# Zeroed dummy matmuls at the start, bf16 rounding sums and merged rotary products in a two-layer Perceiver block

## What is computed

```
x = x + L0_xattn(layernorm(x), ctx)    # 16 heads of 128, inputs rounded to fp8, 512 context keys per batch
x = x + L0_attn(layernorm(x))          # causal convolution, state-space scan
x = x + L0_ffn(layernorm(x))           # 8 experts, top 2
x = x + L1_xattn(layernorm(x), ctx)    # plain attention over the context with a mask
x = x + L1_attn(layernorm(x))          # 16 small heads with rotary positions
x = x + L1_ffn(layernorm(x))           # weights looked up in a 16-entry table
```

```python
def _div_clamp_fp8(x, scale):
    y = jnp.clip(x.astype(jnp.float32) / scale, -FP8_MAX, FP8_MAX)
    y = y.astype(jnp.bfloat16).astype(jnp.float32)
    return y.astype(jnp.float8_e4m3fn).astype(jnp.float32)
```

## Time and profile before

| | us |
|---|---|
| three runs | 454.0, 456.86, 457.67 |
| median | 456.86 |
| the profiled execution | 454.53 |
| its span, first to last instruction | 453.0 |

### The profile page before, as it was taken

How to read it: one execution, slowest core, us unless ns; L and a number is a source line. 1 busy time by engine, 2 the same in 40 slices (tenths; PEclk the granted TensorE clock), 3 DMA queues, 4 the chain that set the end, 5 groups by cost and what they waited for, 6 DMA issues and landing times.

```text
span 453.0 us, 6836 instructions
## 1 busy us (share of the span) xinstructions
PE 422.0 (93%) x2399; PEld 295.6 (65%) x2401; DVE 364.0 (80%) x764; ACT 254.6 (56%) x794; POOL 26.4 (6%) x34
## 2 busy tenths in 40 slices
PE   4999999999999999999999999998987899878587
PEld 1453445777885766767676775876574799836386
DVE  5789999858898879699899988976888799567731
ACT  2468888676545886758987486593113372231150
POOL 0000000000300000101001010100100021000000
PEclk9999999999999999999999999999999899999899
DMA  8268110424001114893446643893558879230000
GB/s 303 116 228 330 35 59 1 187 89 169 1 0 51 43 46 117 172 310 75 116 116 130 171 88 60 199 295 156 113 103 271 322 257 239 55 117 1 2 1 23
DMA packets 14047, 58.57 MB, mean 129 GB/s; under 512 B 1792, under 2 KB 2496, under 8 KB 12480
## 3 DMA queue, kind: packets, MB, share of 16 engines
q1 hardware_dynamic: 10992, 41.66, 25.1%
q0 software_dynamic: 3024, 16.52, 18.5%
HBM read 41.40 MB, written 0.26 MB: 92 GB/s over the span
## 4 chain that ended last, share of the span: by engine, by line
PE 74%; DVE 17%; ACT 4%; issue 2%; DMA 1%; SPq 0%; DVEq 0%; ACTq 0%
PE PS L458 12%; PE PS L431 10%; PE PS L433 9%; PE PS L432 9%; PE PS L1760 4%; PE PS L478 3%; PE PS L1097 3%; DVE small_dt.float L2059 2%; PE PS L1224 2%; PE PS L505 2%; PE PS L1079 2%; PE PS L467 2%; PE PS L1833 1%; PE PS L1082 1%; DMA raw_dt.float<-in_wk_nat 1%
## 5 line engine op out<-in xcount | busy, mean ns | idle before, releaser
L579 ACT ACTIVATE sq_dt.float<-PS 128x128 bf16<-128x128 f32 x256 | 67.1, 278 | 33.5 <-PE PS L433 27.0
L458 PE MATMUL PS<-s_dt.float,ctx_ring_dt.float 128*128 128x512 f32 x128 | 57.7, 593 | 1.3 <-DVE px_dt.float L813 1.3
L431 PE MATMUL PS<-wkc_dt.float32r,ctx_hi_dt.float32r 128*128 128x512 f32 x128 | 53.6, 419 | 0.4
L579 ACT ACTIVATION_READ_ACCUMULATOR sq_dt.float<-PS 128x1 f32 x256 | 53.4, 209 | 0.0
L433 PE MATMUL PS<-wkc_dt.float32r,ctxT_ring_dt.float32r 128*128 128x512 f32 x128 | 50.3, 393 | 0.0
L432 PE MATMUL PS<-wkT_dt.float32r,ctx_hi_dt.float32r 128*128 128x512 f32 x128 | 50.2, 392 | 0.0
L1760 PE MATMUL PS<-wch_dt.float,xs_dt.float 128*128 128x512 f32 x96 | 42.0, 592 | 0.0
L458 PEld LDWEIGHTS PS<-s_dt.float,ctx_ring_dt.float 128*128 128x128 f32 x128 | 23.6, 190 | 25.0 <-issue 23.0
L656 ACT ACTIVATE luttmp_dt.float<-low_bit_dt.float,vec_dt.float,small_dt.float 128x1536 f32<-128x1536 uint8 x24 | 38.5, 1654 | 2.0 <-DMA lutw_dt.float<-luttmp_dt.float 2.0
L663 DVE SCALAR_TENSOR_TENSOR luttmp_dt.float<-idx_dt.float,luttmp_dt.float 128x1536 f32<-128x1536 uint8 x21 | 36.4, 1749 | 0.0
L431 PEld LDWEIGHTS PS<-wkc_dt.float32r,ctx_hi_dt.float32r 128*128 128x128 f32 x128 | 24.0, 188 | 12.2 <-ACT sq_dt.float L579 7.7
(11 more groups left out here) (307 smaller groups left out, 866.2 us busy)
## 6 DMA issues: line engine op xcount, KB each, us to landing
lutw_dt.float<-luttmp_dt.float POOLq DMA_DIRECT2D x21, 768.0 KB, 6.2
wch_dt.float<-in_chunks SPq DMA_DIRECT2D x6, 1024.0 KB, 6.2
ctxT_ring_dt.float<-in_ctxT SPq DMA_DIRECT2D x8, 512.0 KB, 3.4
ctx_ring_dt.float<-in_ctx SPq DMA_DIRECT2D x8, 512.0 KB, 4.0
keysT_dt.float<-in_ctxT SPq DMA_DIRECT2D x8, 512.0 KB, 7.5
keys_dt.float<-in_ctx SPq DMA_DIRECT2D x8, 512.0 KB, 7.6
luttmp_dt.float<-in_idx SPq DMA_DIRECT2D x3, 768.0 KB, 6.0
zu_dt.float<-in_wproj SPq DMA_DIRECT2D x1, 2048.0 KB, 7.3
```

What stands on the lines that cost most here:

```text
L431: nc.tensor.matmul(o, x_hi, hi[:, c, :], start=c == 0, stop=False)
L458: last = nc.tensor.matmul(bank(5 + c), keysr[k][:, t, c * 128:c * 128 + 128], sS[k][:, t, :], start=t == 0, stop=t == KT - 1)
L579: last = nc.scalar.activation(sq[:, (4 * hf + g) * D:(4 * hf + g + 1) * D], bank(hf)[:, g * D:(g + 1) * D], ACT.Square, accum_out=ssq[:, k ...
```

## The change

Four edits, none of which changes what the kernel returns beyond rounding:

1. GpSimd first zeroes 256 fp32 words of the scratch `sq`. TensorE waits for that and not for the constants, runs 14 dummy matmuls of 512 bf16 columns on the zeros, then waits for the constants, transposes x, and runs three dummies of the old kind on the constants.
2. The constant `ROUND` goes from 1.5·2^20 to 1.5·2^4, so that the sum fits bf16, and the sum is written in place over the bf16 value in `round_fp8`, `quantize_values` and `quantize_heads`. In `scaled_input` the difference stays bf16 too, and the multiplication by the input scale reads it and writes fp32. The fp32 scratch `t_q` is gone.
3. As the sum now overwrites a buffer that an earlier difference still reads, VectorE gets waits on its own `catx_ready` and `catc_ready` in `read_values`, `quantize_heads` and `quantize_core`.
4. `pad_half` becomes one copy instead of two, `rotate_keys` one product instead of two, `rotate_queries` one instead of four.

```diff
-ROUND = 1.5 * 2.0 ** 20
+ROUND = 1.5 * 2.0 ** 4
...
         def round_fp8(step, n, dst):
...
             step(nc.vector.tensor_scalar(m_bf[:, 0:n], m_bf[:, 0:n], FP8_MIN_NORMAL, ROUND, ALU.max, ALU.mult))
-            step(nc.vector.tensor_tensor(dst, y_bf[:, 0:n], m_bf[:, 0:n], ALU.add))
-            return nc.vector.tensor_tensor(dst, dst, m_bf[:, 0:n], ALU.subtract)
+            step(nc.vector.tensor_tensor(y_bf[:, 0:n], y_bf[:, 0:n], m_bf[:, 0:n], ALU.add))
+            return nc.vector.tensor_tensor(dst, y_bf[:, 0:n], m_bf[:, 0:n], ALU.subtract)
...
             def read_values(p, hf):
                 dve.wait_ge(v_full, 2 * p + hf + 1)
+                if p or hf:
+                    dve.wait_ge(catx_ready, 2 * p + hf)
...
-                self_step(nc.vector.tensor_tensor(t_q, y_q, m_q, ALU.add))
-                nc.vector.tensor_tensor(dst, t_q.rearrange("p (a q) -> p a q", a=8),
+                self_step(nc.vector.tensor_tensor(y_q, y_q, m_q, ALU.add))
+                nc.vector.tensor_tensor(dst, y_q.rearrange("p (a q) -> p a q", a=8),
...
             def quantize_heads(b, nb, heads):
+                dve.wait_ge(catx_ready, 6 if b == 6 else 7 + heads.start // 8)
...
-                self_step(nc.vector.tensor_tensor(t, y, m, ALU.add))
-                nc.vector.tensor_tensor(catx[:, heads, b * S:(b + 1) * S], t.rearrange("p (a q) -> p a q", a=n),
+                self_step(nc.vector.tensor_tensor(y, y, m, ALU.add))
+                nc.vector.tensor_tensor(catx[:, heads, b * S:(b + 1) * S], y.rearrange("p (a q) -> p a q", a=n),
...
             def pad_half(j):
                 dve.wait_ge(turned, j + 1)
-                o = bank(TURNED[1, j], CT, 128)
-                for c in range(CT):
-                    last = nc.vector.tensor_copy(hpad[:, c, 4 * j:4 * j + 4, 3:S + 3],
-                                                 o[:, c, :].rearrange("p (b s) -> p b s", b=4))
-                return last
+                return nc.vector.tensor_copy(hpad[:, :, 4 * j:4 * j + 4, 3:S + 3], bank(TURNED[1, j], CT, 4, S))
...
             def rotate_keys(j):
...
-                nc.vector.tensor_tensor(k1, o1, cos, ALU.mult)
-                step(nc.vector.tensor_tensor(k2, o2, sin, ALU.mult))
+                both = kr_kt2[:, :, t].rearrange("p a (b s) -> p a b s", b=4)
+                turns = consts[:, CONST["cos"].start:CONST["sin"].stop].rearrange("p (a s) -> p a s", a=2)
+                step(nc.vector.tensor_tensor(both, bank(KEYED[j], 4, 4, S)[:, 0:2],
+                                             turns.unsqueeze(2).broadcast_to([128, 2, 4, S]), ALU.mult))
                 nc.vector.tensor_tensor(kr[:, t], kr[:, t], kt2[:, t], ALU.add)
             def rotate_queries(j):
...
-                for a in range(4):
-                    last = nc.vector.tensor_tensor(qr[:, a, t].rearrange("p (b s) -> p b s", b=4),
-                                                   bank(ASKED[j], 4, 4, S)[:, a], mixed, ALU.mult)
-                last.then_inc(rot_ready, 1)
+                nc.vector.tensor_tensor(qr[:, :, t].rearrange("p a (b s) -> p a b s", b=4), bank(ASKED[j], 4, 4, S),
+                                        mixed, ALU.mult).then_inc(rot_ready, 1)
...
+            pe.wait_ge(warm_ready, 1)
+            for _ in range(14):
+                nc.tensor.matmul(bank(0), sq[:, 0:128], sq[:, 0:512], start=True, stop=True)
             pe.wait_ge(ld_const, 16)
-            keep_clock(2, 0)
             pe.wait_ge(ln_done, 1)
...                                             # four transposes of x
             last.then_inc(x_turned, 1)
+            keep_clock(3, 0)
...
         def _(pool):
             step = Steps(pool, pool_step)
+            nc.gpsimd.memset(buf("sq", 256), 0.0).then_inc(warm_ready, 1)
...
             def scaled_input(n, turned):
...
-                step(round_fp8(step, CT * T, xs[:, n].rearrange("p c t -> p (c t)")))
+                step(round_fp8(step, CT * T, y_bf[:, 0:CT * T]))
                 for c in range(CT):
-                    last = nc.vector.tensor_scalar(xs[:, n, c, :], xs[:, n, c, :], col("in_scale", n * CT + c), None,
+                    last = nc.vector.tensor_scalar(xs[:, n, c, :], yv[:, c, :], col("in_scale", n * CT + c), None,
                                                    ALU.mult)
...
             def quantize_core(n):
                 dve.wait_ge(y_core, n + 1)
+                if n:
+                    dve.wait_ge(catc_ready, n)
```

More of the change, by code:

```diff
@@ L218, in build @@
         low_full, low_read = sem("low_full"), sem("low_read")
+        warm_ready = sem("warm_ready")
         ld_vec, x_turned, x_read, lnT_kept, chunk_read = (sem(n) for n in ("ld_vec", "x_turned", "x_read", "lnT_kept",
@@ L298, in build @@
         y_q, e_q, m_q = (buf("qtmp", 512, skip=256 * i, dtype=bf16) for i in range(3))
-        t_q = buf("qtmp", 512, skip=768)
         def round_fp8(step, n, dst):
@@ L856, in quantize_heads @@
             def quantize_heads(b, nb, heads):
+                dve.wait_ge(catx_ready, 6 if b == 6 else 7 + heads.start // 8)
                 n = heads.stop - heads.start
-                y, e, m, t = (v[:, 0:n * S] for v in (y_q, e_q, m_q, t_q))
+                y, e, m = (v[:, 0:n * S] for v in (y_q, e_q, m_q))
                 self_step(nc.vector.tensor_tensor(y.rearrange("p (a q) -> p a q", a=n), bank(nb, NH, S)[:, heads, :],
@@ L940, in build @@
         kr, kt2 = buf("rotact", T, skip=2048), buf("rotact", T, skip=2304)
+        kr_kt2 = buf("rotact", 2, T, skip=2048)
         vr = buf("rotact", TT, 256, skip=2560)
@@ L1602, in rotate_keys @@
                 dve.wait_ge(qkv_full, 3 * j + 1)
-                k1, k2 = (v[:, t].rearrange("p (b s) -> p b s", b=4) for v in (kr, kt2))
-                o1, o2 = (bank(KEYED[j], 4, 4, S)[:, a] for a in range(2))
-                cos, sin = (const(name).unsqueeze(1).broadcast_to([128, 4, S]) for name in ("cos", "sin"))
-                nc.vector.tensor_tensor(k1, o1, cos, ALU.mult)
-                step(nc.vector.tensor_tensor(k2, o2, sin, ALU.mult))
+                both = kr_kt2[:, :, t].rearrange("p a (b s) -> p a b s", b=4)
+                turns = consts[:, CONST["cos"].start:CONST["sin"].stop].rearrange("p (a s) -> p a s", a=2)
+                step(nc.vector.tensor_tensor(both, bank(KEYED[j], 4, 4, S)[:, 0:2],
+                                             turns.unsqueeze(2).broadcast_to([128, 2, 4, S]), ALU.mult))
                 nc.vector.tensor_tensor(kr[:, t], kr[:, t], kt2[:, t], ALU.add)
@@ L1611, in rotate_queries @@
                 t = slice(128 * j, 128 * j + 128)
-                mixed = const("mixed").unsqueeze(1).broadcast_to([128, 4, S])
+                mixed = const("mixed").unsqueeze(1).unsqueeze(1).broadcast_to([128, 4, 4, S])
                 dve.wait_ge(qkv_full, 3 * j + 2)
-                for a in range(4):
-                    last = nc.vector.tensor_tensor(qr[:, a, t].rearrange("p (b s) -> p b s", b=4),
-                                                   bank(ASKED[j], 4, 4, S)[:, a], mixed, ALU.mult)
-                last.then_inc(rot_ready, 1)
+                nc.vector.tensor_tensor(qr[:, :, t].rearrange("p a (b s) -> p a b s", b=4), bank(ASKED[j], 4, 4, S),
+                                        mixed, ALU.mult).then_inc(rot_ready, 1)
             def rotary_shift(j):
```

## The result

The changed kernel takes **452.62 us** (median of 20 executions, 450.07 to 456.89) against 457.02 us for the kernel before beside it (20 executions, 454.0 to 459.78): ratio **0.993, 95% interval 0.991 to 0.995**. The ratio leaves out one disturbed execution of the changed kernel (456.89 us). It lies near the quotient of the means (452.95 and 456.39 us, 0.992) and not near that of the medians (0.990): by the ratio the gain is 3.3 us, by the medians 4.4. The forecast was 451.8 us with a range of 449.6 to 455.0. The 0.7% of the ratio lies within 1%, to which the prediction gave 0.46, and not above, to which it gave 0.50; by the medians it is 1.0%. The profiled execution took 451.98 us, its span 450.5 us. That is 2.55 us less than the profiled execution before. Where the rest of the gain went is the subject of half the experiments.

What follows compares the result with a forecast made beforehand. It took TensorE as the main bound (74% of the span), with VectorE on the chain mostly from 19 to 63 us. Terms of -3.0, -0.6, -0.2 and -0.5 summed to -4.3 us; forecast 451.8 us, range 449.6 to 455.0.

Steps and rivals of the forecast that it cites:

- The dummies: At the start, early dummies raise TensorE's clock by 8.5 us, so the centring ends at 11.96 instead of 14.95: -3.0 us.
- the bound that the prediction used: At the start, the fourteen dummies end at 7.2 us if TensorE's clock stays low, sooner if it rises under them.
- The rival of the late rise: TensorE's clock rises only in the middle of the centring: half the gain, -1.5 us, giving 453.3 us; chance 12%.
- that of the useless zeros: Zeros do nothing for the clock and the dummies delay the centring 1.1 us: 454.8 us profiled, 457 against the median; 6%.
- going below the median: Forecast set at 451.8 us, between 450.2 from the profiled execution and 452.6 from the median of the runs.
- The bf16 sums: VectorE's sums of 512 columns take 0.43 instead of 0.69 us; `scaled_input` on the chain gives -0.6 us, ends 0 and -0.7.
- capped `scaled_input(2)`: In the front, this call ends in a TensorE wait of only 0.19 us, so no more of its saving passes.
- `quantize_core`, `quantize_values`: In the loop, VectorE saves 2.1 and 1.6 us, but TensorE is busy 99.8% there: 0 on the total.
- `quantize_heads`, the waits and `pad_half`: Shorter 256-column sums with the added waits counted: -0.2 us; one copy instead of two in `pad_half`: -0.08 us twice.
- `rotate_queries`: Behind the loop, one product of 0.69 us replaces four taking 0.87: -0.18 us twice, both on the chain.
- all starts move 4 us, and drops may fall in heavier or lighter stretches: Rival that TensorE's clock drops at another place, near 354 to 358 or 425 us: ±1.5 us on every case; no chance given.
- the forecast sum: All parts together: -3.0 - 0.6 - 0.2 - 0.5 = -4.3 us, 0.9% of the profiled time.

Runs made afterwards that it cites:

- the repeat: The changed kernel, unedited, run once more beside the kernel before: median 452.2 us over six executions, ratio 0.990; its profiled execution took 450.93 us.
- the kernel with the old start: The changed kernel with two dummies on the constants in place of the fourteen on zeros, and without the three before the centring: 454.01 us, ratio 0.996.
- the 52 and 26 above: Executions with a recorded mean granted clock, 52 of the kernel before and 26 of the changed one: at high clock 454.5 and 452.1 us, at low 457.6 and 454.6.
- the version with all of them filled: The changed kernel with the GpSimd mask conversion later and dummies in TensorE's idle gaps behind the loop: median 450.25 us over six executions, ratio 0.985.

## Why the prediction was nearly right

**The dummies: right, size -2.7 for -3.0.** In the profiled execution the rise came earlier than I had to assume, at about 4.1 us, so the dummies ended at 5.82 us and not at 7.2; in the repeat they did end at 7.24 us, the bound that the prediction used, and the centring took the same 3.70 us. The centring went from 6.43 to 3.70 us. I had counted eight intervals of 0.43 us; the step also holds the end of the last product. `scaled_input(0)` was ready at 10.97 us, 0.85 us ahead of need, and VectorE's idle at 16 us was still 0.92 us. The rival of the late rise and that of the useless zeros fell with the weight loads. The rise at 7.05 us in the repeat, 1.3 us ahead of the centring, and the kernel with seven dummies show that the first was not far off. Another 0.40 us of the 3.13 is luck: `wkn` landed that much sooner, and I had said that no edit moves it. For going below the median I had argued that the slow start can be worse in one run than in another; the three traces with a slow centring don't bear that out (6.43, 6.33 and 6.43 us).

**The bf16 sums: mechanism right, front under-sized, -1.0 for -0.6.** The estimate for 512 columns, 0.43 us, was measured as 0.42. The column part halved, 0.53 to 0.27 us for 512 columns, which is the rate that the prediction cited. Wrong were two parts of the step. The multiplications that read bf16 and write fp32 cost nothing extra (350 ns in both kernels, I had put +0.12 on two). And I capped `scaled_input(2)` at the 0.19 us of idle that the trace printed; breaking the transposes there had cost 0.46 us from start to start. The idle printed before a group understated the wait here (0.50 for 0.55 and 0.19 for 0.46 us): the ends of matmuls are modelled and can cover part of it. The starts of the next group tell it.

**`quantize_core`, `quantize_values`: 0, right.** 7.77 us in both, 0.53 us less work a call notwithstanding.

**`quantize_heads`, the waits and `pad_half`: -0.38 for -0.36.** The 256-column sums took 0.29 us for 0.43 (0.30 forecast); with them in fp32 the stretch was 0.21 us longer, which leaves 0.17 for `pad_half` (0.16 forecast). From the first difference to the next read it is 0.74 us before and after, so the added waits cost nothing.

**`rotate_queries`: 0.87 to 0.68 us, as forecast.** The stretch around it is 0.39 us shorter, but the clock moved within it too (0.86 and 0.80 at 420 to 430 us before, 0.56 and 0.75 after), so its share is not shown.

**What failed: "all starts move 4 us, and drops may fall in heavier or lighter stretches", at ±1.5.** The size was fair (+1.64 in the profiled pair), the treatment as luck alone was not enough. I had not asked what the drop at 354 to 358 us held up and what it held back. Reading who released GpSimd's mask conversion (TensorE's third gate and up product) beside VectorE's routing would have shown that full pace in these products brings two engines into one lock, +0.76 us. It is not the moved start that does this: the kernel with the old start did it too. Against the profiled execution the parts give 454.53 - 3.1 - 1.0 - 0.4 - 0.4 = 449.6; with 0.76 and 1.64 given back, 452.0, which is what it took (451.98). Over many executions the change is worth 3.3 us by the ratio and 4.4 by the medians; the forecast sum was 4.3. The sums in the front gave 0.4 us more than that sum has and the centring 0.3 less, and if those executions are like the 52 and 26 above, the 4.4 holds a difference in mean clock which no term of the sum has, so part of the agreement is chance. How often each course occurs in either kernel is open: a course can be told only in a profiled execution, and of the kernel before there is one, of the changed kernel two.

## What to carry to other kernels

Dummy matmuls on a scratch that needs no load are worth their place where the first real products run at half pace; give them enough to come close to the first real work (here fourteen, with gaps of about 1 us behind them; seven, with 2.56 us, were too few), and check the pace at the start by the distance of the weight loads, not by the printed clock. Look at more than one execution: the clock rose at 4.1 us in one and at 7 us in another of the same program. Before you fill TensorE's idle to hold its clock, find every gap of the tail: in two profiles with gaps left the drop only moved on, and the version with all of them filled is the one that came out below the changed kernel on the same chip; and where a drop comes ahead of the filling, the dummies stand in the queue. Compare a single profiled pair only stretch by stretch, since one program can take two courses that differ by 2.4 us in 18.

## What the runs showed of the hardware

- TensorE's clock rose on products of zeros, 14 bf16 products of 512 columns in a row: at about 4.1 us in the changed kernel and at about 7 us in its repeat; in all ten traces that had the fourteen it was up before the centring. The granted clock printed for the first 4 us is 1.00 at half pace.
- A tensor_tensor with all three operands bf16 in SBUF takes 0.29, 0.42 and 0.69 us for 256, 512 and 1024 columns. With an fp32 output it took 0.42, 0.69 and 1.23. "VectorE: DVE Perf Modes" of the Trainium skill (The perf-mode tier table) gives it twice the rate; the columns' part agrees (0.53 to 0.27 us for 512 columns).
- A GpSimd cast or multiplication over 1024 columns (1.04 and 1.05 us) holds up a VectorE product of 16 columns with both inputs in SBUF until it ends: 1.02 and 0.90 us in place of 0.18. A product with one input in PSUM kept its 0.69 us beside such a cast.
- GpSimd's memset of 128x256 fp32 took 0.31 us, within the 0.1 to 0.5 us that the prediction allowed.
